# Mixture-of-experts results added to the output by accumulating scatters, with GpSimd waiting at each new expert

## What is computed

```python
xn = _layernorm(x)                                    # 8192 rows of 128
probs = softmax(xn @ Wr.T)                            # 8 experts
topv, topi = jax.lax.top_k(probs, 2)                  # each row goes to two of them
for e in range(8):                                    # W1[e]: 128x512, W2[e]: 512x128
    y = gelu(xn @ W1[e] + b1[e]) @ W2[e] + b2[e]
    moe += combine[:, e] * y
out = x + attention(xn) + moe
```

## Time and profile before

| | us |
|---|---|
| median of three runs | 848.52 (847.52 to 849.83) |
| the profiled execution, whole | 851.77 |
| its span in the trace | 850.0 |
| PE busy | 699.9 |
| DVE busy | 692.9 |
| POOL busy | 536.0 |
| ACT busy | 525.4 |

### The profile page before, as it was taken

How to read it: one execution, slowest core, us unless ns; L and a number is a source line. 1 busy time by engine, 2 the same in 40 slices (tenths; PEclk the granted TensorE clock), 3 DMA queues, 4 the chain that set the end, 5 groups by cost and what they waited for, 6 DMA issues and landing times.

```text
span 850.0 us, 24989 instructions
## 1 busy us (share of the span) xinstructions
PE 699.9 (82%) x7877; PEld 518.1 (61%) x7878; DVE 692.9 (82%) x1617; ACT 525.4 (62%) x1039; POOL 536.0 (63%) x575
## 2 busy tenths in 40 slices
PE   1366579999999999999888888868999999999800
PEld 1243346666666666666655555537888889888800
DVE  5778878898999998989889999557788888888744
ACT  4541346565656565656556565537989999999800
POOL 8750456767676776767777777334767676667710
PEclk9999899999999999999999999978999999999955
DMA  8294122232323232232233432202222222222189
GB/s 220 80 400 122 64 84 94 81 111 79 114 77 111 80 111 94 94 98 90 84 127 107 139 125 78 64 7 62 84 85 80 85 88 84 82 82 82 56 266 335
DMA packets 113313, 93.66 MB, mean 110 GB/s; under 512 B 16618, under 2 KB 97650, under 8 KB 113268
## 3 DMA queue, kind: packets, MB, share of 16 engines
q1 hardware_dynamic: 95508, 70.26, 27.0%
q0 software_dynamic: 8704, 18.17, 5.9%
q10 hardware_dynamic: 9056, 4.66, 1.9%
HBM read 43.85 MB, written 48.93 MB: 109 GB/s over the span
## 4 chain that ended last, share of the span: by engine, by line
PE 56%; DVE 13%; issue 7%; POOL 7%; DMA 6%; ACT 5%; SPq 5%; DVEq 0%; ACTq 0%; POOLq 0%
PE wide L1259 10%; PE bank_head L1148 7%; PE wide L1113 5%; PE bank_head L1250 5%; PE bank_maxB L1250 5%; PE bank_maxA L1127 4%; PE bank_maxB L1127 3%; DMA xn_rows<-parts_dram 3%; DMA k_cat<-qk_rows 3%; DVE shift L911 3%; POOL probs L581 3%; PE bank_misc L1173 3%; SPq L478 2%; PE bank_maxB L1131 2%; PE bank_maxA L1131 2%
## 5 line engine op out<-in xcount | busy, mean ns | idle before, releaser
L581 POOL TENSOR_SCALAR_AFFINE_SELECT probs<-probs 128x512 f32<-128x512 f32 (+1 forms) x192 | 158.3, 833 | 103.6 <-ACT probs L653 102.8
L653 ACT ACTIVATE probs<-wide 128x1024 f32<-128x1024 f32 x192 | 188.8, 1018 | 47.3 <-PE wide L1117 24.5
L619 POOL DMA_INDIRECT parts_dram<-o_T,dest x144 | 161.0, 1118 | 74.7 <-issue 48.6
L572 POOL DMA_INDIRECT x_slots<-xn_rows,slot_i x128 | 127.3, 995 | 62.8 <-DVE slot_i L868 31.4
L911 DVE TENSOR_REDUCE shift<-bank_maxA 128x2 f32<-128x512 f32 (+1 forms) x192 | 132.1, 688 | 20.1 <-PE bank_maxA L1131 12.9
L911 DVE TENSOR_REDUCE shift<-bank_maxB 128x2 f32<-128x512 f32 (+1 forms) x192 | 131.5, 685 | 4.9 <-PE bank_maxB L1131 0.8
L687 ACT ACTIVATE probs<-wide,b_all 128x256 f32<-128x256 f32 x288 | 121.4, 478 | 16.8 <-PE wide L1259 10.0
L1148 PE MATMUL bank_head<-probs,v_aug 128*32 128x256 f32 (+1 forms) x2048 | 98.9, 334 | 19.1 <-POOL probs L581 18.9
L1259 PE MATMUL wide<-xgT_raw,xnT 128*128 128x256 f16 x864 | 109.2, 277 | 3.7 <-DVE xgT_raw L1020 3.6
L1003 DVE TENSOR_TENSOR probs<-probs 128x512 f16<-128x512 f32 x144 | 99.7, 692 | 5.5 <-ACT probs L693 1.1
L1127 PE MATMUL bank_maxA<-k_cat,q_diag 128*128 128x128 f16 (+1 forms) x512 | 76.2, 252 | 28.5 <-DVE shift L911 19.5
(11 more groups left out here) (174 smaller groups left out, 1252.4 us busy)
## 6 DMA issues: line engine op xcount, KB each, us to landing
qk_rows<-split SPq DMA_DIRECT2D x32, 512.0 KB, 3.2
x_slots<-fill SPq DMA_DIRECT2D x16, 598.5 KB, 7.6
fill<-x_slots SPq DMA_DIRECT2D x72, 133.0 KB
q_diag<-qk_rows SPq DMA_DIRECT2D x256, 32.0 KB
k_cat<-qk_rows SPq DMA_DIRECT2D x64, 128.0 KB
xn_rows<-parts_dram SPq DMA_DIRECT2D x8, 1024.0 KB, 11.8
x_all<-in_x SPq DMA_DIRECT2D x8, 512.0 KB, 7.6
pieces_f<-in_w SPq DMA_DIRECT2D x8, 512.0 KB, 4.8
```

Of the source, the lines that this page charges most:

```text
L572: pool.indirect_dma_start(out=x_slots, out_offset=bass.IndirectOffsetOnAxis(ap=slot_i[:, t, c:c + 1], axis=0), in_=xn_rows[:, t, :], in_of ...
L581: pool.affine_select(out=part, in_=part, compare_op=ALU.is_ge, fill=0.0, base=0, pattern=[[0, n], [1, P]], channel_multiplier=-1).then_inc ...
L619: pool.indirect_dma_start(out=parts_dram, out_offset=bass.IndirectOffsetOnAxis(ap=dest[:, of, t:t + 1].bitcast(U32), axis=0), in_=y[:, of ...
L653: act.activation(probs[:, u, :], ps[:, :], ACT.Exp, scale=SCALE).then_inc(empty, 1)
```

## The change

Three things change together.

First, the results no longer pass through parts_dram. Each of the 144 scatters of POOL adds its 128 rows to the output's rows in DRAM (compute_op add), with the row's number as the index; padded slots have an index past the end and are dropped (bounds_check). The final stage, with SP's loads, DVE's sums and ACT's stores, is gone.

Second, the output must hold the input plus attention before anything is added to it. SP stores each sequence's 256 rows of x_all (128 KB, begin_out) one step after they are done: at the end of steps 5 to 34, and the last two between the first loads of the expert tiles. POOL waits for all 32 stores before its first scatter.

Third, two scatters that add to the same row must not overlap. A row can be in two tiles only when these belong to different experts. So POOL reads the packed expert numbers into a register at the loop's head, works out per tile whether the expert is new, and waits on the landing counts of the three tiles before it: for counts of the round before, long reached, where the expert is the same; for these tiles' own landing where it is new. The slots lose a column (SW), the DVE work on the weights gets smaller, and the counts of placed begin at 16 (FIRST), from the first eight sends to the slots.

```diff
-        parts_dram = nc.dram_tensor("parts_dram", [2 * B * T + NS * S, D], F32).ap()
+        out_rows = out.rearrange("b t d -> (b t) d")
...
+            def begin_out(b):
+                sp.wait_ge(res_ready, b * QT + QT)
+                sp.nop(nofuse=True)
+                sp.dma_start(out[bass.ds(b, 1), :, :].rearrange("a (t p) d -> p (a t) d", p=P),
+                             x_all[:, bass.ds(b * QT, QT), :]).then_inc(out_begun, 16)
+            def stores(s):
+                return 0 <= s - 1 - LAST < B - 2 if isinstance(s, int) else True
...
                         sp.dma_start(q_diag[row:row + 1, 1 - par, :, j, :], shift_T[G * j:G * (j + 1), :]).then_inc(shift_loaded, 16)
+                if stores(s):
+                    begin_out(s - 1 - LAST)
...
-            for c in range(LAST_CHUNKS):
-                if c >= PART_BUFS:
-                    sp.wait_ge(out_ready, c - PART_BUFS + 1)
-                sp.dma_start(parts[:, c % PART_BUFS, :, :], both[:, LC * c:LC * (c + 1), :]).then_inc(parts_loaded[c % PART_BUFS], 16)
...
+            pool.wait_ge(out_begun, 16 * B)
+            def changes_at(i):
+                experts = experts_of(pool, i)
+                steps_up = (experts >> BITS) - (experts & (EVEN + ODD))
+                return (steps_up & EVEN) + EVEN, (steps_up & ODD) + ODD
+            def tile(s, k, changes):
...
+                        for back in range(1, Y_BUFS):
+                            if beyond(u, back - 1):
+                                before = (k - 1 - back) % DEST_BUFS
+                                rounds = (s - k) * 4 - (0 if k >= 1 + back else 32)
+                                pool.wait_ge(placed[before], whole + (rounds + FIRST))
+                    pool.wait_ge(y_ready, u * 2 + 2)
                     pool.nop(nofuse=True)
                     for t in range(2):
-                        pool.indirect_dma_start(out=parts_dram, out_offset=bass.IndirectOffsetOnAxis(ap=dest[:, of, t:t + 1].bitcast(U32), axis=0),
-                                                in_=y[:, of % Y_BUFS, t, :], in_offset=None).then_inc(placed[of], 16)
+                        pool.indirect_dma_start(out=out_rows, out_offset=bass.IndirectOffsetOnAxis(ap=dest[:, of, t:t + 1].bitcast(U32), axis=0),
+                                                in_=y[:, of % Y_BUFS, t, :], in_offset=None, bounds_check=B * T - 1, oob_is_err=False,
+                                                compute_op=ALU.add).then_inc(placed[of], 16)
...
+            for u in range(DEST_BUFS):
+                pool.wait_ge(placed[u], 32 * (NS // DEST_BUFS) + FIRST)
...
-            for c in range(LAST_CHUNKS):
-                act.wait_ge(out_ready, c + 1)
-                act.dma_start(out.rearrange("b (t p) d -> p (b t) d", p=P)[:, LC * c:LC * (c + 1), :],
...
-                V.tensor_tensor(mine[:, :, 0:D], mine[:, :, 0:D], mine[:, :, D:2 * D], ALU.add).then_inc(parts_added, 1)
-                dve.wait_ge(parts_added, c + 1)
-                V.tensor_tensor(here, here, mine[:, :, 0:D], ALU.add).then_inc(out_ready, 1)
```

More of the change, by code:

```diff
@@ L34, in attention_and_moe @@
     NS = B * T * 2 // S + E
-    SW = D + 5
+    SW = D + 4
     NOWHERE = float(1 << 29)
@@ L157, in attention_and_moe @@
         Y_BUFS, DEST_BUFS = 4, 8
+        FIRST = 16
         y = o_T[:, :, :].rearrange("p b (t d) -> p b t d", d=D)
-        spare_row = sb("spare_row", [P, NS * 2])
         dest = sb("dest", [P, DEST_BUFS, 2], I32)
[L161 to L164, removed]
+        chosen = sb("chosen", [P, DEST_BUFS, 2])
         wide = [ctx.enter_context(nc.psum_tensor(f"wide{i}", [P, 1024], F32)) for i in range(2)]
@@ L232, in attention_and_moe @@
         placed = [sem(f"placed{u}") for u in range(DEST_BUFS)]
[L233 to L236, removed]
+        out_begun = sem("out_begun")
         PROJECT, MAXIMA, SOFT, FINISH, LAST = range(5)
@@ L305, in beyond, with steps @@
             return s > n if isinstance(s, int) else True
-        def steps(eng, step, after=((), ()), first_tile=None, written_out=False):
+        assert STAGES % 2 == 1
+        def steps(eng, step, after=((), ()), first_tile=None, written_out=False, in_loop=STAGES - 1):
             experts = None
-            first_whole = STAGES - 1 if not written_out else TAIL
+            first_whole = in_loop if not written_out else TAIL
             count = TAIL - first_whole
@@ L478, in step @@
                         sp.dma_start(q_diag[row:row + 1, 1 - par, :, j, :], shift_T[G * j:G * (j + 1), :]).then_inc(shift_loaded, 16)
-            sp.wait_ge(consts, 25)
+                if stores(s):
+                    begin_out(s - 1 - LAST)
+            sp.wait_ge(consts, 23)
             step(0, 0)
-            sp.wait_ge(consts, 28)
-            steps(sp, step)
+            sp.wait_ge(consts, 26)
+            steps(sp, step, in_loop=STAGES + 1)
             for u in range(2):
-                sp.wait_ge(sent[u], 32 * (NT // 2))
+                sp.wait_ge(sent[u], 32 * (NT // 2 - DEST_BUFS // 4))
+            for u in range(DEST_BUFS):
+                sp.wait_ge(placed[u], FIRST)
             sp.wait_ge(packing, EXPERTS_PACKED)
@@ L497, in tile @@
                 sp.dma_start(xg[:, quad, :, :], x_slots[bass.ds(s * S, S), :].rearrange("(t p) d -> p t d", p=P)).then_inc(xg_loaded[quad], 16)
+                if isinstance(s, int) and s in (1, 2):
+                    begin_out(B - 3 + s)
             tiles(sp, tile, load=False)
-            for u in range(DEST_BUFS):
-                sp.wait_ge(placed[u], 32 * (NS // DEST_BUFS))
-            both = parts_dram[0:2 * B * T, :].rearrange("(t p c) d -> p t (c d)", p=P, c=2)
-            for c in range(LAST_CHUNKS):
-                if c >= PART_BUFS:
-                    sp.wait_ge(out_ready, c - PART_BUFS + 1)
-                sp.dma_start(parts[:, c % PART_BUFS, :, :], both[:, LC * c:LC * (c + 1), :]).then_inc(parts_loaded[c % PART_BUFS], 16)
         @block.gpsimd
@@ L610, in _ @@
             steps(pool, step, written_out=True)
[L612 to L616, removed]
+            pool.wait_ge(out_begun, 16 * B)
+            EVEN = sum((E - 1) << BITS * j for j in range(0, FIELDS - 1, 2))
+            ODD = sum((E - 1) << BITS * j for j in range(1, FIELDS - 1, 2))
+            def changes_at(i):
+                experts = experts_of(pool, i)
+                steps_up = (experts >> BITS) - (experts & (EVEN + ODD))
+                return (steps_up & EVEN) + EVEN, (steps_up & ODD) + ODD
@@ L625, in _ @@
+            changes = changes_at(0)
+            for s in range(UNROLL):
+                tile(s, s, changes)
+            with pool.Fori(0, NS // UNROLL - 1) as i:
+                changes = changes_at(i + 1)
+                for k in range(UNROLL):
+                    tile(i * UNROLL + (UNROLL + k), k, changes)
+            tile(NS, 0, changes_at(NS // UNROLL))
+            for u in range(DEST_BUFS):
+                pool.wait_ge(placed[u], 32 * (NS // DEST_BUFS) + FIRST)
         @block.scalar
@@ L709, in tile @@
                     before = (k - 2 - Y_BUFS) % DEST_BUFS
-                    later(act, placed[before], (s - k) * 4 + (32 if k >= 2 + Y_BUFS else 0), beyond(s, 1 + Y_BUFS))
+                    later(act, placed[before], (s - k) * 4 + (32 + FIRST if k >= 2 + Y_BUFS else FIRST), beyond(s, 1 + Y_BUFS))
                     act.wait_ge(xg_used, s * 2 - 2)
```

41 lines of the change are left out of this document (18 added, 23 removed).

## The result

The changed kernel takes 899.2 us (median of four runs, 897.6 to 902.4) beside 849.2 us for the kernel before on the same chip: 1.059 times as long, interval 1.055 to 1.063. That is slower by 50 us, and outside the range of 810 to 868 us. The profiled execution took 897.63 us, 895.9 of them its span.

What follows compares the result with a forecast made beforehand. It took PE to bound the tiles, POOL nearly full, and DMA traffic the end. From 851.8 us: 37.9 off for the end, 11 on for stores, 3 on for POOL, 3.25 off for the median: 825 us, range 810 to 868.

Steps and rivals of the forecast that it cites:

- the price of the adding scatter: POOL in the tiles: an adding scatter was taken to cost POOL what a plain one does, 0.96 us by the median.
- The dearer scatter: Rival, POOL in the tiles: adding scatters take longer and set the pace, 14.4 us per 0.1 us each; chance 0.34.
- the sum's 3 us in the tiles: Expert tiles: POOL needs 225 of 227 us, so part of its late waits stays, 3 us lost (0 to 20).
- Seven waits at 2.3 us: POOL at each new expert: the next scatter waits for the last one's landing, 16 us in all (13 to 30).
- Loop heads: POOL at the tile loop's head: nine reads of the packed experts at 0.5 us, 4.5 us (0 to 13).
- The register arithmetic: POOL's register work per tile: hidden beneath the scatters as the sequencer runs ahead; without that cover, 29 us.
- The stores: SP in the attention: 27 stores ahead of a half's loads delay k_cat, 0.42 us a step, 11 us lost (0 to 26).
- the slack of 0.09 us: Attention seam: time that SP's chain from the shifts to k_cat has to spare against PE's, taken off each store's 0.51 us.
- The end: After the last scatters: parts loads, sums and stores go, only an adding scatter's landing stays; 37.9 us gained (35.9 to 38.4).
- Free stores: Rival, attention: PE's stand at m6 is made good later in the step, stores cost nothing, 811 us; chance 0.13.
- Serial additions: Rival, tiles: a DMA engine adds rows one by one, deciding from 0.19 us a row; 897 us at 0.25; chance 0.07.
- A wait at every tile: Rival, POOL in the tiles: landings are awaited for the same expert too, 65 more waits of 2.3 us, about 970 us; chance 0.03.

## Why the prediction was wrong

**What failed: the price of the adding scatter.** The sum took 0.96 us "if an adding scatter costs POOL what a plain one does", and 204 us for scatters and gaps, 161.0 of them scatters. The scatters alone took 231.2 us. I had no row of an adding one, and took as nearest row the sends to the slots, from which I argued that "what a row holds hardly counts". That is true (half the columns change nothing), but it is no evidence on the addition: the sends are plain scatters too. They bound the price by length and say nothing of its kind. With GpSimd at 225 of 227 us by my own sum, the verdict hung on this one unseen number, and a chance of 0.34 for it to be dearer was too low for that.

**The rival that came true.** The dearer scatter was priced at 14.4 us for each 0.1 us. At the measured 1.544 us this makes 825 + 5.84 x 14.4 = 909 us; 899 came. That the two are so near is in part luck: the rival puts 84 us on top of the sum's 3 us in the tiles, where 61.9 came, since the mean rose less than the median and GpSimd had idle time to fill; the stores and the end were 11 us dearer than the sum had them. The mechanism (GpSimd sets the pace, ACT waits for landings) is in the rows above; my range ended at 1.26 us, with nothing behind that end but a weight. The reason that I gave for it could fit a small part only. The Trainium skill ("GPSIMD Engine Reference", section "4. When to use GPSIMD") has one core write the read descriptors and another the write descriptors, from which I had guessed twice the rows to write on the first. The runs show 1.8 ns a row with the addition and 1.0 without; that would fit the guess, but it is 0.10 of 0.57 us. What the fixed 0.47 us are stays open.

**The rest of GpSimd's sum held.** Seven waits at 2.3 us beyond a gap, 16 us: measured 15.0. Gaps of 0.30 us, 43 us: 41.5, and the waits in place of seven of them. Loop heads, 4.5 us: nothing, since no other gap is longer than 0.31 us. The register arithmetic is hidden, as the sequencer runs ahead. And where the scatter is plain (the run without the addition) the loss in the tiles is 0, not 3 us; there its end at 0 was the right one.

**The stores: right in kind, short in size.** The late k_cat and the waits of PE in most steps came as foretold, but 17.5 us and not 11. The term that failed is 0.51 us a step, built from one seam. From the end of the shifts to the next q_diag load it is 0.58 us at that seam. But in the loop over the steps two kinds alternate, and I had read one of them only. The other kind in the kernel before:

```profile
277.26 2.44 SPq L478 DMA_DIRECT2D q_diag<-shift_T  x4
279.88 1.72 SPq L437 DMA_DIRECT2D q_diag<-qk_rows  x4
```

There it is 0.18 us. After the change the two kinds take 1.61 (302.28 to 303.89) and 1.00 us (287.59 to 288.59), so the store costs 1.03 and 0.82 us: 0.42 for the issue, and the rest for the wait and the registers around it, of which I had counted 0.15. In the last eight of the 27 steps, behind the loop, it costs 0.51 to 0.55 us, as I had it. Seam by seam through both timelines, the 27 together are 21.5 us longer than before, 0.80 us each in place of 0.51. Less the slack of 0.09 us this makes 27 x 0.71 = 19 us, beside the 17.5 here and the 19.2 of the stores alone; single executions tell no more, so the slack may stand. The forecast's bound of 0.61 us a step was passed, its bound with the data's traffic (26 us) was not, though the traffic cost nothing that shows.

The rule that I had set against the row is the Trainium skill's ("DMA: Bandwidth & Descriptors", section "Issuing engines are not separate DMA queues"): only the issuer's sequencer time matters. The runs agree with that: moving the issue alone gave 14.6 us back. But what the page calls "usually small" was 17.5 us here, because the issue stood in front of a load that PE waits for.

**The end: 33.5 us, not 37.9.** I let the span end 2.8 us behind the last scatter's start (a plain landing and 0.5 us). It ended 7.2 us behind it. The landing was no dearer than I took it: the last scatters land 2.7 us after their issue. The other 4.5 us are nearly all one row of GpSimd's instruction queue, a DRAIN, which is not counted as busy (count, ns min/median/max, first and last start), in the kernel before and now:

```profile
L44 POOLq DRAIN  x1: 6273/6273/6273, 807.7 to 807.7; - x1
```

```profile
L44 POOLq DRAIN  x1: 3991/3991/3991, 891.7 to 891.7; - x1
```

When the last scatter has landed, the DRAIN at the end of GpSimd's program runs 3.99 us, from 891.7 to 895.7, and the span ends at 895.9. Before, it was over at 814.0, beneath the load of the parts, and cost nothing; the span then ended 0.4 us after the last store landed (846.43 and 3.2 us). The failed step is that I took the landing for the end of the span and gave GpSimd's closing no time, though the trace of before has it (the row is a part of it). Little of it is the addition's: without that the DRAIN takes 3.66 us and the piece 6.3 us (827.1 to 833.4). What GpSimd does in it stays open; with half the rows it takes 3.09 us (adding) and 2.52 (plain), with half of each row 3.99.

**The other rivals.** *Free stores*: no, unless they are moved, and then nearly (2.9 us; 0.2 us in the run without the addition). *Serial additions*: no. From 610 to 870 us the queue of the scatters reads:

```profile
q0 software_dynamic: 18432, 8.10, 34.5%
```

That is 0.345 x 260 x 16 / 18432 = 0.078 us a packet, well under the 0.19 us at which the rival decides; and half the data changed nothing. *A wait at every tile*: no; its price of 2.3 us was right, as the run with it shows.

## What to carry to other kernels

An instruction that does more than the one in the trace has no price until it is measured; a row that varies another property (here the row's length) is no bound for it, and where the engine is nearly full, the range must reach to where that price decides. Replacing a stage by work in a loop that runs beside it is worth what the loop's own engine has to spare: the additions put 75 us on GpSimd, and the 62 of them that showed ate the 33.5 us saved at the end, and more. What an engine does behind its last work counts as soon as the program ends with that engine. A DMA issue on a chain of loads can cost its wait and registers as well as its issue, as the stores did; put it in front of a wait in which the issuer idles, and read every kind of seam before pricing it.

## What the runs showed of the hardware

- An accumulating scatter from SBUF to DRAM rows holds GpSimd 1.544 us by the median where a plain one takes 0.972 (128 rows of 512 bytes, both with a bound). By a straight line through 64 and 128 rows, 0.47 us of the difference do not depend on the rows. The adding one takes 1.544 us with rows of half the length too.
- It goes out as 144 packets (20,736 of the 24,832 of the whole run, since 128 plain sends make 32 each, which is 4,096), where a plain scatter makes 32 (8,704 for 272 of them in the kernel before). With half the rows it is 80 (15,616 in that run), so one a row and 16 more; the plain one stays at 32. The DMA engines are busier, 0.48 in place of 0.28, with less data moved.
- It lands 3.3 us after its issue by the median, 2.7 us where the queue is nearly empty at the end; the plain one took 2.3 us there.
- Rows that the bound drops save GpSimd nothing: the last five tiles hold only padding by the reference's router, and their scatters take the same 1.54 us by the median. From 874.5 us on the queue moves 0.01 MB, in 1,296 packets, which is 144 for each of nine scatters still.
- GpSimd's closing DRAIN takes 3.99 us behind the landing of the last adding scatter and 3.66 behind a plain one (2.52 with half the rows).
